# Row sums from a 33rd column of ones, transposes in two halves through one bank, mask products in two row halves, and another order at the start

## The reference

```python
x = x + tanh(g_xattn) * xattn(layernorm(x), ctx, Wq, bq, Wk, bk, Wv, bv, Wo, bo)
x = x + tanh(g_ffn) * ffn(layernorm(x), gate, up, down)
# xattn, per image and head:
dots = einsum('bhdt,bhdtw->bhtw', qh, k_win) * scale   # 16 positions in the window
attn = softmax(dots, axis=-1)
out  = einsum('bhtw,bhdtw->bhdt', attn, v_win)         # then Wo, bo
# ffn: silu(x @ gate) * (x @ up) @ down, each weight (int - zero) * scale by groups of 128 rows
```

## Time and profile before

| | |
|---|---|
| median of 3 runs | 1634.97 us (1632.92 to 1637.67) |
| the profiled execution, its own time | 1636.69 us |
| its span, first to last instruction | 1634.9 us |
| PE busy | 1554.2 us (95%) |
| DVE busy | 1455.4 us (89%) |
| ACT busy | 1049.9 us (64%) |
| POOL busy | 1288.5 us (79%) |
| attention stage | up to about 429 us, where the first product of L1189 starts |

### The profile page before, as it was taken

How to read it: one execution, slowest core, us unless ns; L and a number is a source line. 1 busy time by engine, 2 the same in 40 slices (tenths; PEclk the granted TensorE clock), 3 DMA queues, 4 the chain that set the end, 5 groups by cost and what they waited for, 6 DMA issues and landing times.

```text
span 1634.9 us, 40568 instructions
## 1 busy us (share of the span) xinstructions
PE 1554.2 (95%) x16614; PEld 810.4 (50%) x16614; DVE 1455.4 (89%) x1429; ACT 1049.9 (64%) x1187; POOL 1288.5 (79%) x945
## 2 busy tenths in 40 slices
PE   5899999998789999999999999999999999999996
PEld 3566666676434444444444444444444444444444
DVE  4688878887599999999999999999999999999997
ACT  4577777776456666666666666666666666666652
POOL 3576766776778888888888888888888888888865
PEclk9899999999899999999999999999999999999999
DMA  4666655655366766666666666666666776667579
GB/s 120 152 157 146 174 136 148 175 146 131 104 155 155 153 154 148 152 153 153 152 152 153 153 155 155 155 154 150 153 149 147 156 155 152 152 154 155 116 180 322
DMA packets 193139, 252.66 MB, mean 155 GB/s; under 512 B 14542, under 2 KB 138126, under 8 KB 192938
## 3 DMA queue, kind: packets, MB, share of 16 engines
q1 hardware_dynamic: 168186, 163.74, 35.1%
q0 software_dynamic: 23616, 85.99, 30.0%
q10 hardware_dynamic: 1152, 0.33, 0.1%
HBM read 113.92 MB, written 16.78 MB: 80 GB/s over the span
## 4 chain that ended last, share of the span: by engine, by line
PE 88%; issue 3%; POOL 2%; SPq 2%; DMA 1%; DVE 1%; ACT 1%; ACTq 0%; DVEq 0%; POOLq 0%
PE bank L1189 68%; PE bank L1098 3%; PE bank L1087 3%; PE bank L1130 2%; PE bank L1050 2%; PE bank L1061 2%; PE bank L1046 2%; PE bank L1054 2%; PE bank L1108 1%; PE bank L1077 1%; PE bank L1058 1%; PE bank L1066 1%; POOL oacc L618 1%; SPq L392 1%; DMA gates<-in_g_ffn_dram 1%
## 5 line engine op out<-in xcount | busy, mean ns | idle before, releaser
L974 DVE SCALAR_TENSOR_TENSOR acc<-bank,scale,acc 128x1024 f32<-128x1024 f32 x784 | 969.8, 1279 | 49.6 <-PE bank L1189 10.8
L1189 PE MATMUL bank<-xT,w_int 128*128 128x512 f16 x3584 | 846.4, 379 | 10.2 <-DVE xT L925 4.6
L618 POOL TENSOR_TENSOR oacc<-oacc,d_part 128x1024 f32<-128x1024 f32 x225 | 550.4, 2450 | 55.4 <-ACT d_part L811 49.3
L1189 PEld LDWEIGHTS bank<-xT,w_int 128*128 128x128 f16 x3584 | 349.9, 98 | 434.5 <-DVE xT L925 6.2
L811 ACT ACTIVATE d_part<-bank,scale 128x1024 f32<-128x1024 f32 x225 | 250.9, 1115 | 205.3 <-PE bank L1189 201.3
L1189 PE MATMUL bank<-h_hi,d_int 128*128 128x512 f16 x896 | 339.6, 379 | 3.8 <-ACT acc L785 1.8
L1189 PE MATMUL bank<-h_lo,d_int 128*128 128x512 f16 x896 | 339.6, 379 | 0.0
L811 ACT ACTIVATE d_more<-bank,scale 128x1024 f32<-128x1024 f32 x164 | 182.8, 1115 | 156.2 <-PE bank L1189 156.2
L620 POOL DMA_DIRECT2D oacc<-d_more x164 | 155.0, 945 | 116.2 <-ACT d_more L811 109.9
L560 POOL TENSOR_TENSOR raw_z<-raw_w,raw_z 128x512 int32<-128x512 int32 x168 | 225.2, 1341 | 8.8 <-DMA raw_z<-in_L_ffn_gate_z_dram 5.3
L686 ACT ACTIVATE pT<-bank 96x1024 f16<-96x1024 f16 x128 | 123.5, 1018 | 32.8 <-PE bank L1098 32.4
(11 more groups left out here) (86 smaller groups left out, 1512.6 us busy)
## 6 DMA issues: line engine op xcount, KB each, us to landing
oacc<-d_more POOLq DMA_DIRECT2D x164, 512.0 KB, 5.0
raw_w<-in_L_ffn_gate_w_dram SPq DMA_DIRECT2D x56, 256.0 KB, 3.6
raw_z<-in_L_ffn_gate_z_dram SPq DMA_DIRECT2D x56, 256.0 KB, 4.3
raw_w<-in_L_ffn_up_w_dram SPq DMA_DIRECT2D x56, 256.0 KB, 3.4
raw_z<-in_L_ffn_up_z_dram SPq DMA_DIRECT2D x56, 256.0 KB, 4.0
raw_w<-in_L_ffn_down_w_dram SPq DMA_DIRECT2D x56, 256.0 KB, 3.0
raw_z<-in_L_ffn_down_z_dram SPq DMA_DIRECT2D x56, 256.0 KB, 3.7
vt<-vn_hl SPq DMA_DIRECT2D x64, 192.0 KB
```

The source lines that it names most:

```text
L618: nc.gpsimd.tensor_tensor(into, into, d_part[:, (n - 1) % 2, :], ALU.add).then_inc(d_added, 1)
L974: nc.vector.scalar_tensor_tensor(out=into, in0=pair[u % 4][:, :, :].rearrange("p h r -> p (h r)"), scalar=scale[:, par, i, m, k:k + 1], in ...
L1189: last = nc.tensor.matmul(dst[:, h, :], weights, rows_of(h, part), start=(part == 0), stop=(part == 1))
```

## The change

1. **Row sums.** Each value strip gets a 33rd column of ones (`V1` = 33; `vn_hl`, `vt` and the padding are laid out with 33 columns for each head). `mix` makes 33 columns for each head, at a distance of 64 in banks 6 and 7; the last of them is the row sum. `add_up` is gone from PE with its waits, and the reciprocal moves from the middle of `soften` into `take_mix`.
2. **Banks.** Since `mix` takes two banks, the third bank of the task ring is now bank 4, and the transposes have bank 5 alone. `turn_probs` and `take_pT` are done in halves `hg` = 0 and 1, and each half waits until the one before it has been copied out.
3. **Orders in step n, after.** PE: `scores(n)`, first and second tasks, `turn_probs(n-1, 0)`, `mix(n-2)`, third tasks, `turn_probs(n-1, 1)`. ACT: (`norm_x`), first tasks, `exp(n)`, second tasks, `take_pT(n-1, 0)`, third tasks, `take_pT(n-1, 1)`, (`norm_row`). DVE: `soften(n)`, first and second tasks, `take_mix(n-2)`, third tasks, (moments).
4. **Mask products.** Each of the two takes only 64 rows of the array, one the lower half and one the upper, with `spread` and `window` built for both (6 more small selections on POOL at the start).
5. **The start.** tanh of the gates comes after the first tasks; four of the eight transfers of `move_k(0)` are issued by ACT; the bias vectors are loaded ahead of x of image 1; the transposes of the scale tables come after the first `scores`.

```diff
+    V1 = 2 * HD + 1
+    VS = 64
...
-        proj, score, mixed = (bank[0], bank[1], bank[7]), bank[2:4], bank[6]
-        turned = [half[:, :].bitcast(fp16) for half in bank[4:6]]
+        proj, score, mixed = (bank[0], bank[1], bank[4]), bank[2:4], bank[6:8]
+        turned = bank[5][:, :].bitcast(fp16)
...
-            def take_pT(n):
-                act.wait_ge(probs_turned, n + 1)
-                for hg in range(2):
-                    last = nc.scalar.activation(pT[0:2 * KW, n % 2, hg, :], turned[hg][0:2 * KW, :], ACT.Copy)
-                last.then_inc(pT_ready, 1)
+            def take_pT(n, hg):
+
+                act.wait_ge(probs_turned, 2 * n + hg + 1)
+                nc.scalar.activation(pT[0:2 * KW, n % 2, hg, :], turned[0:2 * KW, :], ACT.Copy).then_inc(pT_ready, 1)
...
-            act.wait_ge(gates_loaded, 32)
-            nc.scalar.activation(tanh_g[:, :], gates[:, :], ACT.Tanh).then_inc(gates_ready, 1)
             norm_x(0)
             act.wait_ge(bias_loaded, 48)
-            for t in first_tasks[:4]:
+            for t in first_tasks[:2]:
+                take_high(*t)
+
+            act.wait_ge(emptied_proj, low_done("k", 0, 1))
+            act.wait_ge(km_zeroed[0], 1)
+            for h in range(HG):
+                lo = GC + HD * h
+                act.dma_start(km[0][lo:lo + HD, :, h, PAD:PAD + T], k_hl[lo:lo + HD, :, :]).then_inc(k_moved, 16)
...
                     exp(n)
-                    for t in second + third:
+                    if n == 0:
+                        keep_scales()
+                    for t in second:
                         take_high(*t)
                     if n:
-                        take_pT(n - 1)
+                        take_pT(n - 1, 0)
+                    for t in third:
+                        take_high(*t)
+                    if n:
+                        take_pT(n - 1, 1)
...
                 nc.vector.tensor_reduce(rmax[:, buf], all_scores, AX.X, ALU.max).then_inc(max_ready, 1)
-                if n >= 3:
-                    invert_sums(n - 3)
                 dve.wait_ge(max_ready, n + 1)
...
+                nc.vector.reciprocal(rinv[:, n % 2], all_mixed[:, :, 2 * HD]).then_inc(sums_inverted, 1)
...
-                    for t in first:
+                    for t in first + second:
                         take_low(*t)
                     if n >= 2:
                         take_mix(n - 2)
-                    for t in second + third:
+                    for t in third:
                         take_low(*t)
...
-                    nc.tensor.matmul(score[hg][:, 0:JQ * KW].rearrange("p (x k) -> p x k", k=KW), spread[:, :],
-                                     window[:, :].unsqueeze(1).to_broadcast([P, JQ, KW]),
+                    r = slice(GC * hg, GC * hg + GC)
+                    nc.tensor.matmul(score[hg][:, 0:JQ * KW].rearrange("p (x k) -> p x k", k=KW), spread[r, :],
+                                     window[r, :].unsqueeze(1).to_broadcast([GC, JQ, KW]),
...
-            def turn_probs(n):
+            def turn_probs(n, hg):
+
                 pe.wait_ge(p_lo, n + 1)
-                if n:
-                    pe.wait_ge(pT_ready, n)
-                for hg in range(2):
-                    for x in range(JQ):
-                        at = (hg * JQ + x) * 2 * KW
-                        last = nc.tensor.transpose(turned[hg][:, x * P:(x + 1) * P], p_hl[:, n % 2, at:at + P], ident16[:, :])
+                if n or hg:
+                    pe.wait_ge(pT_ready, 2 * n + hg)
+                for x in range(JQ):
+                    at = (hg * JQ + x) * 2 * KW
+                    last = nc.tensor.transpose(turned[:, x * P:(x + 1) * P], p_hl[:, n % 2, at:at + P], ident16[:, :])
                 last.then_inc(probs_turned, 1)
...
                     if n:
                         pe.wait_ge(shifted, n)
-                    if n >= 3:
-                        add_up(n - 3)
                     scores(b, s)
...
                     first, second, third = tasks_of(b, s)
                     for t in first + second:
                         project(*t)
+                    if n == 1:
+                        pe.wait_ge(s_kept, 2)
+                    if n:
+                        turn_probs(n - 1, 0)
                     if n >= 2:
                         mix(n - 2)
                     for t in third:
                         project(*t)
-                    if n == 1:
-                        pe.wait_ge(s_kept, 2)
                     if n:
-                        turn_probs(n - 1)
+                        turn_probs(n - 1, 1)
```

More of the change, by code:

```diff
@@ L380, in load_ctx, with move_k @@
                 sp.dma_start(ct[:, :], ctx_in[b]).then_inc(ctx_loaded, 16)
-            def move_k(b):
+            def move_k(b, halves=(0, 1)):
                 sp.wait_ge(emptied_proj, low_done("k", b, 1))
@@ L389, in move_k @@
                 for h in range(HG):
-                    for hg in range(2):
+                    for hg in halves:
                         lo = GC * hg + HD * h
@@ L430, in _ @@
             sp.dma_start(d_stage[0:F // P, :], down_s).then_inc(s_loaded, 16)
-            move_k(0)
+            move_k(0, (0,))
             load_ctx(1)
+            sp.wait_ge(ones_placed, 2)
             place_v(0)
@@ L565, in _ @@
                                     base=0, pattern=[[-1, P]], channel_multiplier=1).then_inc(masks_made, 1)
[L566 to L578, removed]
+            made = 1
@@ new lines, in _ @@
+            for lo in (0, GC):
+                for jj in range(JJ):
+                    at = spread[lo:lo + QB, QB * jj:QB * jj + QB]
+                    if made > 1:
+                        pool.wait_ge(masks_made, made)
+                    nc.gpsimd.affine_select(out=at, in_=at, compare_op=ALU.not_equal, fill=1.0, base=0,
+                                            pattern=[[-1, QB]], channel_multiplier=1).then_inc(masks_made, 1)
+                    made += 1
+                win = window[lo:lo + QB, :]
+                nc.gpsimd.affine_select(out=win, in_=win, compare_op=ALU.is_ge, fill=MASKED, base=0,
+                                        pattern=[[1, KW]], channel_multiplier=-1).then_inc(masks_made, 1)
+                made += 1
+                pool.wait_ge(masks_made, made)
+                nc.gpsimd.affine_select(out=win, in_=win, compare_op=ALU.is_ge, fill=MASKED, base=WIN - 1,
+                                        pattern=[[-1, KW]], channel_multiplier=1).then_inc(masks_made, 1)
+                made += 1
@@ L766, in _ @@
                         cast_piece(0, s - 1, 0)
-            take_pT(S * B - 1)
+            take_pT(S * B - 1, 0)
+            take_pT(S * B - 1, 1)
             for t in end_tasks:
@@ L882, in soften @@
                                         ALU.subtract).then_inc(shifted, 1)
[L884 to L888, removed]
             def take_mix(n):
@@ L911, in take_low @@
                 if kind == "v":
-                    hi, lo = (vn_hl[:, 4 * n:4 * n + 4, :, part, :] for part in range(2))
+                    hi, lo = (vn_hl[:, 4 * n:4 * n + 4, :, HD * part:HD * part + HD] for part in range(2))
                     nc.vector.tensor_tensor(lo, src.rearrange("p (n h d) -> p n h d", h=HEADS, d=HD), hi,
@@ L1147, in _, with turn_scales @@
             pe.wait_ge(wo_loaded, 32)
-            nc.tensor.matmul(mixed[:, 0:1], wo[:, :], bv_col[:, :], start=True, stop=True).then_inc(bias_turned, 1)
-            pe.wait_ge(s_loaded, 48)
-            for n in range(F // P):
-                last = nc.tensor.transpose(bank[5][:, n * 2 * NK:(n + 1) * 2 * NK], gu_stage[0:2 * NK, n * P:(n + 1) * P],
-                                           ident[0:2 * NK, 0:2 * NK])
-            for n in range(NCT):
-                last = nc.tensor.transpose(bank[4][:, n * (F // P):(n + 1) * (F // P)],
-                                           d_stage[0:F // P, n * P:(n + 1) * P], ident[0:F // P, 0:F // P])
-            last.then_inc(s_turned, 1)
+            nc.tensor.matmul(mixed[0][:, 0:1], wo[:, :], bv_col[:, :], start=True, stop=True).then_inc(bias_turned, 1)
+            pe.wait_ge(zeroed, 2)
+            pe.wait_ge(masks_made, 2 + 2 * (JJ + 2))
+            def turn_scales():
+                pe.wait_ge(s_loaded, 48)
+                for n in range(F // P):
+                    last = nc.tensor.transpose(bank[5][:, n * 2 * NK:(n + 1) * 2 * NK], gu_stage[0:2 * NK, n * P:(n + 1) * P],
+                                               ident[0:2 * NK, 0:2 * NK])
+                for n in range(NCT):
+                    last = nc.tensor.transpose(bank[7][:, n * (F // P):(n + 1) * (F // P)],
+                                               d_stage[0:F // P, n * P:(n + 1) * P], ident[0:F // P, 0:F // P])
+                last.then_inc(s_turned, 1)
             for b in range(B):
@@ L1172, in _ @@
                         project(*t)
-                    if n == 1:
-                        pe.wait_ge(s_kept, 2)
                     if n:
```

(8 more changed lines are left out.)

92 lines of the change are left out of this document (37 added, 55 removed).

## The result

The changed kernel takes 1664.72 us in the median (1664.18 to 1671.26), the kernel before 1634.52; the ratio is 1.018, with a 95% interval from 1.0156 to 1.0204. Its profiled execution has a span of 1663.4 us against 1634.9.

The account below looks back on a forecast made before the run. PE's own sequence was taken as the bound before, a closed circle through PE, ACT, DVE and POOL after. 1636.7 us +29 (circle) +6 (issue) +7 (clock) -4 (start), median 1.7 lower: forecast 1672 us, range 1650 to 1705.

Parts of the forecast that it names:

- The bound before: From 60 to 402 us PE's own sequence was the limit, 5.56 us a step, with slack in every other engine.
- the other circle: Waits over moments, norm_x and the steps of one image, in the kernel before: near 20.5 us, below PE's 22.
- The closed round: Scores, subtraction, exp, first pT copy, second transposes, next scores wait on one another: 5.37 to 5.99 us a step, 23.2 an image.
- The longer circle: After the change, waits from moments_x through norm_x, exp, copies and moments_row round one image: 25.9 us an image.
- The 32 us that PE would save: Gain if PE stayed the bound: 58 steps, each 0.40 us from add_up and 0.16 from the mask products.
- The sum, +29: The attention steps from 60 to 402 us: 371 us for 58 steps against 342, so 29 us more.
- Issue waits and clock, +13: In the attention steps: issue waits falling on the circle +6, half-clock PE after idles in s = 1 +7.
- The start, -4: Before 60 us: the queue to the third ctx starts about 4 us earlier; bounds -8 and 0.
- After 402 us, 0: The stretch after the attention steps: no change, range -2 to +4 us.
- The plain round alone: Rival: in the attention steps the longer circle does not close; about 1636 us, no change; chance 0.11.
- PE as the bound: Rival: the first half's copy is done when PE reaches the second; -32 and -4, 1600 us; chance 0.07.
- The low clock over most of steps 0 and 1: Rival: in every image projections take twice as long; some 3 us an image more, 1710 to 1720; chance 0.14.

Follow-up runs that it names:

- the kernel with few sums: The kernel before with one product for the row sums of each step in place of 16; 1620.23 us, ratio to before 0.9896.
- the kernel with the halves alone: The kernel before with only the transposes done in halves through bank 5, with their orders on PE, ACT and DVE; 1678.95 us, ratio to before 1.0266.
- the mask alone: The kernel before with only the mask products done in two row halves; ratio to before 1.0004.

## Why the prediction was right, and where its terms were off

The forecast was 1672, the result 1664.7, slower as foreseen, and by the mechanism foreseen. Point by point:

- **The bound before** (PE's own sequence). Right: shown by the kernel with few sums, 17 of 21 us, and 0.37 of 0.37 in a clean step. But the other circle lay closer to it than "near 20.5": the terms named there, 0.96 once and 1.07 + 0.45 in the two rounds that the circle holds, make 4.0 and not 5.5, so 21.9 us against PE's 22.
- **The closed round.** Right, and shown from both sides: put into the kernel before it costs 45 us, opened in the changed kernel it gives 26 back.
- **The longer circle, 25.9 us an image.** Right in kind; a clean image took 26.38. The largest part of the difference is one term: half the transposes, 0.45 in the sum, took 0.54 to the next mask (276.45 to 276.99), and the mask 0.27 for 0.25, in the two rounds that the circle holds 0.22 us. I had written that the change of mode "hides in the 0.41 us"; that step failed. It does not hide, it costs 0.07 to 0.10 us. Next to it, the first half's copy took 1.15 us to the transposes (275.30 to 276.45) for 1.07, in two rounds 0.16.
- **The 32 us that PE would save.** The mask's 0.16 a step was over twice too much (0.05 to 0.07 once the change of mode is paid); the sums' part held (the few sums). The 33rd column costs PE nothing: the 64 products of mix take 0.59 us to the next row's start with 32 columns and 0.59 or 0.60 with 33 (273.44 to 274.03).
- **The sum, +29.** Here is a slip: from the mask of step 5 at 59.71 to that of step 62 are 57 steps, not 58. The sum for 57 steps would have been about 6.6 us less, 364.5, and +22. The measured stretch is 378.3, +36. The 14 us between are the clean image, longer than the sum (26.38 for 25.9, about 6 us over the 12 images 3 to 14, half of it the mode changes), issue waits and the clock in these (4), and images 1, 2 and the last, taken too light (4). The last line has a slip too: 1636.7 + 38 less 1.7 is 1673, not 1672.
- **Issue waits and clock, +13.** Too much: 4 to 5 in the trace (26.76 - 26.38 = 0.38 an image). The slow clock came more often than reckoned, and cost far less: from 60 to 430 us 10 of 56 score groups took over 1.1 us in place of 0.85, all in steps s = 1, where I had taken half of these. But I had taken 1.1 us for each, as not covered by any wait; the masks of those steps (images 4 to 7 and 10 to 14) stand 6.98 to 7.37 us apart for 6.97 in a clean one, 0 to 0.4 more. The wait of rmax for the moments covered most of the rest: in image 13 the slow scores end at 379.26, the moments after them, and rmax starts at 379.54. So the stretch was forecast 6 us too long (+42 for +36): some 16 too much by the slip and by this term, some 10 too little by the clean image and the light images. The total is closer than the terms.
- **The start, -4.** -2.5 in this trace; alone 5.6 by the times (2 to 9) and 4.4 in its trace.
- **After 402 us, 0.** Missed: -5.8. In the kernel before PE stood still for 3.75 and 3.17 us there, the first "issue", the second a wait for POOL, and ran slow after it; in the kernel after the longest such wait is 2.74. Why it came out better was not tested.
- **The rivals.** The plain round alone (1636) and PE as the bound (1600) are out. The low clock over most of steps 0 and 1 (1710 and over) is out too: 0.95 over the stretch.

## What to carry to other kernels

An engine that has slack in busy time can still be part of a round. Before splitting a transfer between two engines into halves that share one buffer, follow what stands ahead of the copy in the other engine's order: here a copy behind `exp`, and with it the next scores. With the second half placed behind the next scores, 26 of the 30 us came back, and with `norm_x` moved as well the kernel was 8 us faster than before; that is still less than the 17 us of the sums and the 6 us of the start that each gave alone, so part of the cost stays. Start-to-start distances of rows, added round such a circle, gave the period of a clean image within 2%; counting the work of each engine gave the opposite sign.

## What the runs showed of the hardware that I had not expected

- Going from full-width products to products on 64 rows cost 0.07 to 0.10 us on PE (0.48 against 0.40 from sums to mask, 0.54 against 0.44 from transposes to mask), over half of what halving the mask gained. Going from eight transposes to the 96 x 32 products of mix shows the same price: 0.54 us, against 0.44 to the sums (both in the kernel with the halves alone, medians of 50 and 49 steps).
- The length of the last wait alone does not tell whether the clock falls. With no wait over 1.7 us it stayed at 1.00 over 342 us, but by the earlier trace rows it was at half after 1.64. In the kernel after, the scores ran at full clock after a wait of 2.35 us, and in another image at half after 1.24, with one of 0.95 for "issue" shortly before (292.97):

```profile
243.09 0.61 PE L1109 MATMUL bank<-ident,p_hl 128*128 128x128 f16 x8 [2.35 <-ACT pT L692]
...
243.89 0.86 PE L1098 MATMUL bank<-km,q_hl 64*32 64x192 f16 x64
...
295.87 1.01 PE L1109 MATMUL bank<-ident,p_hl 128*128 128x128 f16 x8 [1.24 <-ACT pT L692]
...
297.24 1.48 PE L1098 MATMUL bank<-km,q_hl 64*32 64x192 f16 x64
```

  What exactly decides stays open.
- Waits for "issue" differ from build to build and image to image: 23 us in the kernel before, 31 with the mask alone, 7 in the kernel after, where the waits for ACT may cover them.
